# Decoder layer on one core: the first head group's rotation in PSUM and its first head stacked without DRAM

## The reference

```python
q = (x @ Wq + bq).reshape(B, S, H, D)      # B, S, H, D = 4, 512, 16, 32
k = (x @ Wk + bk).reshape(B, S, H, D)
v = (x @ Wv + bv).reshape(B, S, H, D)
q, k = _apply_rope(q, cos, sin), _apply_rope(k, cos, sin)   # x*cos + swapped pairs*sin
scores = einsum('bshd,bthd->bhst', q, k) / sqrt(D)          # causal mask, softmax
out = einsum('bhst,bthd->bshd', softmax(scores), v).reshape(B, S, E) @ Wo + bo
x = _layernorm(x + out)
```

## Time and profile before

| | us |
|---|---|
| median of three runs | 991.81 |
| lowest, highest | 990.37, 994.39 |
| the profiled execution | 994.69 |
| its span in the trace | 992.9 |

### The profile page before, as it was taken

How to read it: one execution, slowest core, us unless ns; L and a number is a source line. 1 busy time by engine, 2 the same in 40 slices (tenths; PEclk the granted TensorE clock), 3 DMA queues, 4 the chain that set the end, 5 groups by cost and what they waited for, 6 DMA issues and landing times.

```text
span 992.9 us, 16198 instructions
## 1 busy us (share of the span) xinstructions
PE 942.6 (95%) x5272; PEld 763.6 (77%) x5272; DVE 729.0 (73%) x1588; ACT 514.8 (52%) x1150; POOL 596.0 (60%) x645
## 2 busy tenths in 40 slices
PE   7888999999999978997899999999999999999997
PEld 5666887777787756886788888888878878888885
DVE  5556778768877876676777677677787877777767
ACT  4566777767777776654543333433443354333333
POOL 2466645845764645456656656657855876665644
PEclk9987999999999999999899999999999999999999
DMA  5975665866666690012100110110201023011002
GB/s 225 243 192 149 182 160 160 256 159 170 171 197 176 190 297 3 22 44 107 64 1 33 64 64 33 65 64 32 64 33 64 33 106 106 33 64 64 33 32 85
DMA packets 40739, 105.20 MB, mean 106 GB/s; under 512 B 4944, under 2 KB 5072, under 8 KB 38608
## 3 DMA queue, kind: packets, MB, share of 16 engines
q1 hardware_dynamic: 40656, 104.16, 35.3%
HBM read 78.98 MB, written 25.17 MB: 105 GB/s over the span
## 4 chain that ended last, share of the span: by engine, by line
PE 71%; POOL 8%; ACT 7%; DVE 7%; issue 5%; DMA 2%; SPq 0%; POOLq 0%; DVEq 0%; ACTq 0%
PE pd L706 25%; PE pj L654 14%; PE pj L706 9%; PE pg L706 5%; PE pu L706 5%; PE pv L697 4%; PE ps L669 3%; PE pb L682 2%; PE pa L682 2%; ACT prob L896 1%; DVE prob L1156 1%; PE ps L654 1%; DMA qk_scratch<-raw 1%; POOL raw L1450 1%; ACT raw L886 1%
## 5 line engine op out<-in xcount | busy, mean ns | idle before, releaser
L1156 DVE CUSTOM_DVE_ANT_0 prob<-ps,mask 128x512 f32<-128x512 f32 (+3 forms) x256 | 124.6, 489 | 87.6 <-PE ps L669 81.1
L896 ACT ACTIVATE prob<-prob,nmax 128x512 f32<-128x512 f32 (+3 forms) x256 | 144.0, 563 | 85.2 <-DVE nmax L1156 83.4
L669 PE MATMUL ps<-ks,qs 128*128 128x256 f32 (+2 forms) x256 | 106.3, 417 | 6.4 <-DVE nmax L1156 4.5
L1617 POOL TENSOR_TENSOR g_lo<-gated,g_hi 128x512 fp32r<-128x512 f32 x32 | 49.5, 1546 | 90.5 <-ACT g_hi L1000 90.5
L1450 POOL TENSOR_TENSOR raw<-raw,cos 128x512 f32<-128x512 f32 x32 | 42.2, 1318 | 96.0 <-DVE pj L1138 80.4
L1288 DVE TENSOR_TENSOR xb<-pd,xb 128x512 f32<-128x512 f32 x116 | 79.4, 685 | 26.7 <-PE pd L706 26.7
L1610 POOL TENSOR_TENSOR wop_lo<-wsum,wop_hi 128x512 fp32r<-128x512 f32 x64 | 81.6, 1296 | 1.3 <-ACT wop_hi L985 1.3
L1000 ACT CAST g_hi<-gated 128x512 fp32r<-128x512 f32 x32 | 19.9, 622 | 118.3 <-DVE gated L1348 118.3
L706 PE MATMUL pd<-dn_hi,g_hi 128*128 128x512 f32 x244 | 75.4, 390 | 1.6 <-issue 1.0
L706 PE MATMUL pd<-dn_hi,g_lo 128*128 128x512 f32 x244 | 75.2, 389 | 0.0
L706 PE MATMUL pd<-dn_lo,g_hi 128*128 128x512 f32 x244 | 75.1, 389 | 0.0
(11 more groups left out here) (525 smaller groups left out, 2824.6 us busy)
## 6 DMA issues: line engine op xcount, KB each, us to landing
f_raw<-in_w_ffn SPq DMA_DIRECT2D x32, 768.0 KB, 4.1
qs<-qk_scratch SPq DMA_DIRECT2D x64, 256.0 KB, 4.6
ks<-qk_scratch SPq DMA_DIRECT2D x60, 256.0 KB, 7.1
qk_scratch<-qk_hi SPq DMA_DIRECT2D x32, 256.0 KB, 2.0
qk_scratch<-raw SPq DMA_DIRECT2D x32, 256.0 KB, 2.0
res<-in_x SPq DMA_DIRECT2D x4, 1024.0 KB, 5.1
x_scratch<-res SPq DMA_DIRECT2D x4, 1024.0 KB, 5.3
xb<-x_scratch SPq DMA_DIRECT2D x4, 1024.0 KB, 5.9
```

The source lines that it names most:

```text
L669: pe.matmul(ps[:, t % 2, 0:w], qs[n % 2][:, r, s * P:(s + 1) * P], ks[n % 2][:, r, 0:w], start=True, stop=True).then_inc(s_done, 1)
L896: act.activation(prob[:, t % PROBS, 0:w], prob[:, t % PROBS, 0:w], ACT.Exp, bias=nmax[:, n % 2, i:i + 1], scale=-1.0, accum_out=rsum[:, n ...
L1156: dve.tensor_tensor_reduce(prob[:, t % PROBS, 0:w], ps[:, t % 2, 0:w], mask[:, S - w:S], -D ** -0.5, 3e38, ALU.add, ALU.min, accum_out=nma ...
L1617: pool.tensor_tensor(lo, (gated, gated_b)[b][:], hi.bitcast(F32), ALU.subtract).then_inc((glo_done, glo_b_done)[b], 1)
```

## The change

- The rotation of group 0 (q and k) is one block on DVE in slot -21, where only k's steps stood before: swap q, sin q, swap k, add q, sin k, add k. Swap and sin product lie in the PSUM banks `pa` (q) and `pb` (k), not in `swp`.
- `store` for group 0 also copies the first head (32 partitions of `qk_hi` or `raw`) straight from SBUF into `qs0` and `ks0`, four copies each; `first_stack` reads only the other three heads. `first_q` is two semaphores: PE waits for the first at tile 0 and for the second at tile 4. ACT waits for the copies before it writes `raw` for group 1.
- v2 is in slots 0 to 2 and v3 in slots 5 to 7, four matmuls a slot. "b" is in slots 14 to 17.
- The rotation, split and store of k of group 1 come six slots later (`turned`), group 1's stack at slot 7.
- The loads of Wo and of the fourth weight block come after that stack, at slot 7, Wo first. The fourth block is split in slot 14, Wo in 18, 20, 23 and 25. DVE's part of the third block's split goes from slot -8 to 1, `spread_bias` from -7 to 4.

```diff
--- before.py
+++ after.py
@@ -53,8 +53,8 @@
 ROTATE, ADD, SPLIT_QK = 1, 3, 5
 AV, RECIPS, NORMALIZE, SPLIT_O = 20, 21, 25, 26
 BEGIN = -29
-SPLIT_W = {(1, 0): (-22, -20), (2, 0): (-8, -8)}
-SPLIT_LATE = {(3, 0): 8, ("o", 0): 10, ("o", 1): 12, ("o", 2): 14, ("o", 3): 17}
+SPLIT_W = {(1, 0): (-22, -20), (2, 0): (-8, 1)}
+SPLIT_LATE = {(3, 0): 14, ("o", 0): 18, ("o", 1): 20, ("o", 2): 23, ("o", 3): 25}
 LOAD_X = (10, 11, 28, 29)
 SPLIT_X = (27, 28, 34, 35)
 
@@ -113,10 +113,11 @@
         out.append((("q", n), TILES * n - 29, (3, 3, 3, 3)))
         out.append((("k", n), TILES * n - 24, (4, 4, 4)))
         out.append((("r", n), TILES * n + RECIPS, (4,)))
-    out.append((("b", 0), 11, (1, 1, 1, 1)))
+    out.append((("b", 0), 14, (1, 1, 1, 1)))
     for b in range(B):
         for s in range(ST):
-            out.append((("v", ST * b + s), TILES * G * b - 21 + (0, 4, 16, 20)[s], (3, 3, 3, 3)))
+            if b or s < 2:
+                out.append((("v", ST * b + s), TILES * G * b - 21 + (0, 4, 16, 20)[s], (3, 3, 3, 3)))
             out.append((("o", ST * b + s), TILES * G * b + (75, 79, 91, 95)[s], (3, 3, 3, 3)))
     chain, t = [], SCORES
     for name in CHAINS.split():
@@ -127,6 +128,7 @@
         chain.append(((key[0], int(key[1:])), t, (3 * KT if key[0] in "mo" else 4 if key[0] in "taur" else LENGTHS[key[0]],), int(at)))
         t += LENGTHS[key[0]]
     late = {unit[0] for unit in chain}
+    chain += [(("v", 2), 0, (4, 4, 4), 0), (("v", 3), 5, (4, 4, 4), 1)]
     out = [unit + (pj_bank(unit[0], unit[1]),) for unit in out if unit[0] not in late] + CROSS + chain
     return sorted(out, key=lambda unit: unit[1])
 
@@ -149,6 +151,11 @@
 SPLIT_W1, SPLIT_W2, SPLIT_LOW_W = (ENDS["m", 8] - 3, ENDS["m", 11] + 4), (ENDS["t", 15] + 2, ENDS["m", 12]), (ENDS["m", 8] + 2, ENDS["m", 12])
 SPLIT_DN = (ENDS["a", 15] + 8, ENDS["a", 15] + 12)
 SUMS = (ENDS["m", 4] + 17, ENDS["m", 5] + 17, ENDS["u", 5] + 2, ENDS["u", 8] + 2)
+
+
+def turned(n, u, k):
+
+    return ENDS["qk"[u], n] + k + (6 if (n, u) == (1, 1) else 0)
 
 
 def hop(key, k):
@@ -272,7 +279,7 @@
     qkhi_done, qklo_done = sem("qkhi_done"), sem("qklo_done")
     stored = [sem(f"stored{u}") for u in range(2)]
     stacked = [sem(f"stacked{u}") for u in range(2)]
-    first_q, first_k = sem("first_q"), [sem(f"first_k{r}") for r in range(4)]
+    first_q, first_k = [sem(f"first_q{r}") for r in range(2)], [sem(f"first_k{r}") for r in range(4)]
     v_done = sem("v_done")
     s_done, max_done, exp_done, t_done = (sem(f"{n}_done") for n in ("s", "max", "exp", "t"))
     a_moved, b_moved, c_moved = (sem(f"{n}_moved") for n in "abc")
@@ -399,6 +406,12 @@
         def store(n, u, lo):
 
             rows = (4 * n + 2 * lo + u) * P
+            if n == 0:
+                sp.wait_ge((qkhi_done, qklo_done)[lo], u + 1)
+                for j in range(4):
+                    if lo == (j // 2 if u == 0 else j % 2):
+                        head = raw[0:D, u, :] if lo else qk_hi[0:D, u, :].bitcast(F32)
+                        sp.dma_start((qs0, ks0)[u][D * j:D * j + D, 0, :].bitcast(F32), head).then_inc((first_q, first_k)[u][0], 16)
             if lo:
                 sp.wait_ge(qklo_done, 2 * n + u + 1)
                 sp.dma_start(scratch[rows:rows + P, :], raw[:, u, :]).then_inc(stored[u], 16)
@@ -469,12 +482,12 @@
 
             for u in range(2):
                 sp.wait_ge(stored[u], 32)
-                for r in range(1 if u == 0 else 4):
+                for r in range(1, 2 if u == 0 else 4):
                     for j in range(4):
                         rows = (2 * (j // 2 if u == 0 else j % 2) + u) * P
                         if u == 0:
-                            sp.dma_start(qs0[D * j:D * j + D, :, :].bitcast(F32),
-                                         scratch[rows:rows + P, :].rearrange("(r d) s -> d r s", d=D)).then_inc(first_q, 16)
+                            sp.dma_start(qs0[D * j:D * j + D, 1:4, :].bitcast(F32),
+                                         scratch[rows + D:rows + P, :].rearrange("(r d) s -> d r s", d=D)).then_inc(first_q[1], 16)
                         else:
                             sp.dma_start(ks0[D * j:D * j + D, r, :].bitcast(F32),
                                          scratch[rows + D * r:rows + D * r + D, :]).then_inc(first_k[r], 16)
@@ -493,18 +506,18 @@
         for t in range(BEGIN, END):
             for n in range(GROUPS):
                 for u in range(2):
-                    if t == ENDS["qk"[u], n] + SPLIT_QK:
+                    if t == turned(n, u, SPLIT_QK):
                         store(n, u, 0)
-                    if t == ENDS["qk"[u], n] + SPLIT_QK + 1:
+                    if t == turned(n, u, SPLIT_QK + 1):
                         store(n, u, 1)
-                if t == TILES * n - 13:
+                if t == TILES * n - (9 if n == 1 else 13):
                     if n:
                         stack(n)
                     else:
                         first_stack()
-            if t == -12:
+            if t == 7:
+                load_w("o")
                 load_w(3)
-                load_w("o")
             b, at = t // (TILES * G), t % (TILES * G)
             if t >= 0 and b < B - 1 and at in LOAD_X:
                 load_x(KT * (b + 1) + LOAD_X.index(at))
@@ -660,8 +673,8 @@
             if t % TILES == 0 and n:
                 pe.wait_ge(stacked[n % 2], 128 * ((n + 1) // 2))
             if n == 0 and t % ST == 0:
-                if t == 0:
-                    pe.wait_ge(first_q, 64)
+                if r < 2:
+                    pe.wait_ge(first_q[r], 64)
                 pe.wait_ge(first_k[r], 64)
             if t >= 2:
                 pe.wait_ge(max_done, t - 1)
@@ -878,6 +891,8 @@
                 act.copy(vg[n // ST % 2][:, n % ST, :], src).then_inc(v_done, 1)
             else:
                 u = "qk".index(kind)
+                if n == 1:
+                    act.wait_ge((first_q, first_k)[u][0], 64)
                 if n:
                     act.wait_ge(stored[u], 32 * n)
                 else:
@@ -1120,7 +1135,7 @@
         def first_add(u):
             dve.wait_ge(cos_done, u + 1)
             dve.wait_ge(sin_done, u + 1)
-            dve.tensor_tensor(raw[:, u, :], raw[:, u, :], swp[:], ALU.add).then_inc(rot_done, 1)
+            dve.tensor_tensor(raw[:, u, :], raw[:, u, :], swapped(0, u), ALU.add).then_inc(rot_done, 1)
 
         def split_x(k):
 
@@ -1129,19 +1144,17 @@
 
         def swapped(n, u):
 
-            return over[PLACE["qk"[u], n][0]] if in_bank(n) else swp[:]
+            return over[PLACE["qk"[u], n][0]] if n else (pa, pb)[u][:]
 
         def swap(n, u):
             dve.wait_ge(raw_done[u], n + 1)
-            if not in_bank(n) and n + u:
-                dve.wait_ge(rot_done, 2 * n + u)
             dve.stream_shuffle(swapped(n, u), raw[:, u, :], SWAP).then_inc(swap_done, 1)
 
         def times_sin(n, u):
-            if in_bank(n):
+            if n:
                 dve.wait_ge(rot_done, 2 * n + u)
             dve.wait_ge(swap_done, 2 * n + u + 1)
-            dve.tensor_tensor(swp[:], swapped(n, u), sin[:], ALU.mult).then_inc(sin_done, 1)
+            dve.tensor_tensor(swp[:] if n else swapped(0, u), swapped(n, u), sin[:], ALU.mult).then_inc(sin_done, 1)
 
         def row_max(t):
 
@@ -1397,12 +1410,18 @@
                 recips((t - AV) // TILES)
             for n in range(GROUPS):
                 for u in range(2):
-                    if t == ENDS["qk"[u], n] + ROTATE:
+                    if n and t == turned(n, u, ROTATE):
                         swap(n, u)
-                    if t == ENDS["qk"[u], n] + ROTATE + 1:
+                    if n and t == turned(n, u, ROTATE + 1):
                         times_sin(n, u)
-                    if n == 0 and t == ENDS["qk"[u], n] + ADD:
-                        first_add(u)
+            if t == ENDS["k", 0] + ROTATE:
+                swap(0, 0)
+                times_sin(0, 0)
+                swap(0, 1)
+                first_add(0)
+                times_sin(0, 1)
+                first_add(1)
+            for n in range(GROUPS):
                 if t == (TILES * n + NORMALIZE if n < GROUPS - 1 else hop(("r", n), 0) + 3):
                     normalize(n)
             for n in range(B * ST):
@@ -1413,7 +1432,7 @@
             for (n, k), (_, at) in SPLIT_W.items():
                 if t == at:
                     split_w(n)
-            if t == -7:
+            if t == 4:
                 spread_bias()
             if t == ENDS["b", 0] + 1:
                 add_bias()
@@ -1625,11 +1644,11 @@
                     root1(n)
             for n in range(GROUPS):
                 for u in range(2):
-                    if t == ENDS["qk"[u], n] + ROTATE:
+                    if t == turned(n, u, ROTATE):
                         times_cos(n, u)
-                    if n and t == ENDS["qk"[u], n] + ADD:
+                    if n and t == turned(n, u, ADD):
                         add(n, u)
```

(2 more changed lines are left out.)

## The result

The changed kernel takes 997.92 us (median, 997.15 to 1000.45) beside 991.69 for the kernel before (989.76 to 994.99): ratio 1.0059, interval 1.0046 to 1.0073. It is slower by 6 us, where +0.9 was forecast and a range up to 996.9; slower by more than 5 us had been given a chance of 0.11. A second series gave 1.0056 (1.0042 to 1.0069). The profiled execution took 997.92, its span is 996.1, against a span of 992.9: the two profiles differ by 3.2 us, half of what the medians differ by.

The account below looks back on a forecast made before the run. PE, busy 95% of the span, bounds it; gains come only where PE stands still or runs at lower clock. -1.0 + 1.9 = +0.9 us on 994.69 gives 995.6, less 2.9 to the median: 992.7 us, range 988.3 to 996.9.

Parts of the forecast that it names:

- Part 1: Group 0's rotation in PSUM: k rotated 4.1 us sooner, PE ends the projections at 25.8 us, 0.9 earlier.
- Part 2: First head copied SBUF to SBUF: lands near 24.4 us, before PE needs it; tile 0 moves from 33.06 to 25.8.
- Part 3: Slots 0 to 13 on PE: new wait of 2.6 us for V's eviction (1.6 to 3.7); slot 14 at 46.4.
- Part 4: Group 1's stack first read at 38.7; Wo lands at 52.3, PE waits 5.9 us; tile 21 at 65.5.
- Part 5: Wo's third and fourth splits on POOL in slots 23 and 25 delay tile 21 to 36 by 1.9 us.
- Rival (a): At slot 14, Wo doesn't hold PE: tile 16 at 49.1, tile 21 at 59.2, total 986.4 us; chance 0.12.
- (b): Stalls as forecast, but POOL has room and the Wo splits cost nothing: -1.0, 990.8 us; chance 0.2.
- (d): Something else holds slot 0: tile 0 stays near 31, about +3, 994.8 us; chance 0.05.
- (c): At slot 14, Wo lands later, at 54.3, PE waits 8 us and resumes at 1.2 GHz: +5.5, 997.3 us; chance 0.13.
- The sum: From Wo's landing to tile 21 on PE: 10.6 us of work plus 2.6 of lower clock.
- the gain of 1.0: Tile 21 was to start at 65.5 us, 1.0 us earlier than in the kernel before.
- 2 either way for the clock: Allowance in the forecast's range for time PE runs at the lower clock: 2 us each way.

Follow-up runs that it names:

- wo_late: Changed kernel with Wo's third and fourth splits in slots 37 and 39 instead of 23 and 25: 997.23 us, ratio 1.0041.
- warm_after: Changed kernel with 24 unread matmuls in slot 14, ahead of the wait for Wo: 994.88 us, ratio 1.0014.
- b_late: Changed kernel with the bias product in slots 27 to 30 and its spread in slot 26: 994.93 us, ratio 1.0024.
- before_p2: Kernel before, unchanged, run again for another profile: 990.87 us.
- w3_b_late: Changed kernel, bias product in slots 27-30, Wo's last splits in 37 and 39, third block's in -16 and -15, fourth block's load in -12: 985.00 us, ratio 0.9938.

## Why the prediction was wrong

**Held, nearly to the number.** Part 1: DVE's adds and split, k rotated at 17.9 (forecast 18.5), k's add 0.69 and not 1.77 (a POOL split ran from 17.18 on, beside it), tile 0 at 25.3 (25.8). Part 2: the copies landed 0.2 us late for PE, next to no cost. Part 3: the new wait of q for V's eviction was 2.14 (2.6, bounds 1.6 to 3.7), PE at slot 14 at 45.6 (46.4). Part 4: first read of the stack at 38.07 (38.7), Wo there at 52.4 (52.3), PE's wait 6.49 (5.9). Part 5: 20.77 - 19.10 = 1.7 us more from tile 21 to 36 (1.9), shown by wo_late. Rival (a) fell, as Wo did hold PE; (b) fell by wo_late; (d) fell by tile 0; and (c), whose 997.3 us is close to the time measured, fell too, as Wo landed at 52.4 and not behind 53.5.

**Missed, 1: from Wo to tile 21.** The sum had 10.6 us of work and 2.6 of clock; it took 14.7. The clock was right (2.9 lost while busy, 2.8 by warm_after), and so was the work: without the fall of the clock the way took 11.9 us in warm_after, 10.65 without the wait of 1.25 us that the sum had missed. q of group 3 uses the bank of the bias product and waits for DVE to empty it (62.30 above; b_late doesn't have it). Before, four slots lay between the two units, and now there is one. Tile 21 came 1.7 us later than forecast, and the gain of 1.0 became a loss of 0.7.

**Missed, 2: behind tile 36.** I carried the difference to the end unchanged. From tile 36 to 48 it took 19.1 us instead of 18.5, and 0.3 us more came by the end, 0.9 in all; the second stretch at half clock, 85 to 93, covers the weighted sums of group 1. Where no stretch lies between these two tiles, as in before_p2 and w3_b_late, it took 17.3 and 17.6.

**Missed, 3, the largest: from the profile to the median.** The step "That run lies 2.9 above the median of the three, 991.81, which gives 992.7" took what made that run slow to be the same for both kernels, and subtracted it from the forecast too. It was not the same. The changed kernel's profiled run had no such surplus: it was at its median, its second profile looked the same, and of the 6.2 us between the medians 3.0 are this step. In the prediction's terms, tile 21 was to gain 2.6 us of clock, because before lost 5.2 us ahead of it and the changed kernel would lose 2.6. But ahead of tile 21 the two other profiles of before lost nothing and 1.7 us: a faster run of before doesn't have that half clock to give. Clocks of 0.87 and 0.80 in the two stretches that mattered, in a run 3 us above its median, should have made me ask whether those stretches belong to the kernel. Range and chances suffered for the same reason, as "2 either way for the clock" was centred on a run at the slow end.

The sum with these: +0.9, +1.7 for tile 21, -0.2 for part 5, +0.9 behind tile 36 give +3.3, against 3.2 by the profiles; +3.0 for the state of the profiled run gives 6.3, against 6.2 by the medians. That it comes out so well is partly by construction, since the terms were read from the two profiles that it compares.

What is shown and what isn't: that the stretches of before stand in some of its runs only, and that the profiles with fewer are shorter by 2.6 and 3.8 us, mostly ahead of tile 48, is shown. That half clock makes all of the 3.0 us is argued. From tile 16 to 21, where only the first profile has a stretch, it accounts for 1.6 and 1.9, and over the 72 runs time and mean clock go together only loosely. For the changed kernel the fall behind the wait for Wo is in both its profiles, and its six runs of the second series have mean clocks of 0.982 to 0.984, but it was not seen in each run. What sets a stretch off is open: ahead of tile 0, PE waited about 1.4 us for the sin product in all three profiles of before, then 1.12, 0.91 and 0.62 for k, and the clock fell behind these waits only in the first.

## What to carry to other kernels

A gain at the head of a pipeline is worth what the next resource in the order can take: here 7.7 us at the first tile were taken back by a load that was put behind a 2 MB stack, and by a consumer that stayed near it. When a load is deferred, move its first consumer by as much, and look at each in-order engine that touches it. And before a sum is made against one profiled run, see whether the waits and half-clock stretches in it belong to the kernel or to that run: if its time is not the median's, the difference lies somewhere in the trace.

## What was not expected of the hardware

The same kernel had between 1.7 and 9.0 us of PE's work at 1.2 GHz in its first 90 us, in three executions with the same instructions. 5.6 us of matmuls that nobody reads, put into a wait, made the kernel about 4 us faster. The Trainium skill (TensorE: Matmul & The Clock Gate, Part 1: The HAM clock gate) says that the clock falls when the array stands still and that where a change of level comes differs from run to run. For the first, PE of the changed kernel stood still from 46.0 us on, and its granted clock was 0.99 from 47 to 48 and 0.50 from 48 on. For the second, three profiles of the kernel before have their first stretch at 33, 76 and 47 us.
